# Two starts and one seam of a three-attention program: initial loads without barriers, setup and first item of the closing stream inside the batch before it

## The reference, cut to what matters

```
x = x + mla_0(layernorm(x))        # latent attention, 16 heads: the first pass of mla_sublayer
x = x + ternary(layernorm(x))      # x @ w_ste.T + bias, w_ste from round(w / mean|w|)
x = x + gated_delta(layernorm(x))  # convolved q, k, v and a recurrence over tokens
x = x + ternary(layernorm(x))
x = x + mla_1(layernorm(x))        # second pass of mla_sublayer
x = x + ffn(layernorm(x))          # the closing stream: attention that modulates a gated MLP
x = x + rotary(layernorm(x))       #                     16 heads of 16, rotary positions
x = x + ffn(layernorm(x))
```

## Time and profile before

| what | value |
|---|---|
| median of three timed runs | 3333.66 us |
| profiled execution, its own time | 3329.28 us |
| its span | 3327.5 us |
| TensorE busy | 3193.5 us, 96% |
| VectorE, ScalarE, GpSimd busy | 72%, 59%, 25% |
| DMA moved | 66.84 MB, mean 20 GB/s |

### The profile page before, as it was taken

How to read it: one execution, slowest core, us unless ns; L and a number is a source line. 1 busy time by engine, 2 the same in 40 slices (tenths; PEclk the granted TensorE clock), 3 DMA queues, 4 the chain that set the end, 5 groups by cost and what they waited for, 6 DMA issues and landing times. The chain is left out here.

```text
span 3327.5 us, 89349 instructions
## 1 busy us (share of the span) xinstructions
PE 3193.5 (96%) x34218; PEld 2639.1 (79%) x34218; DVE 2411.1 (72%) x7923; ACT 1955.1 (59%) x4769; POOL 827.1 (25%) x828
## 2 busy tenths in 40 slices
PE   6999989999999999999999969999799999999999
PEld 5888878888888888888888858788667777777787
DVE  4777778777778878787878637777666777777764
ACT  3565556666666666666666626565465555555553
POOL 2333322232222223232322223333200111111100
PEclk9999999999999999999999979999999999999999
DMA  6000000000000000000000040000000000000000
GB/s 242 1 1 1 1 8 27 22 21 18 15 18 25 18 25 18 22 16 21 21 22 21 9 163 1 1 1 1 1 1 1 1 1 1 1 5 5 5 8 10
DMA packets 51337, 66.84 MB, mean 20 GB/s; under 512 B 4962, under 2 KB 40290, under 8 KB 49378
## 3 DMA queue, kind: packets, MB, share of 16 engines
q1 hardware_dynamic: 50914, 61.13, 5.8%
HBM read 58.56 MB, written 2.56 MB: 18 GB/s over the span
## 5 line engine op out<-in xcount | busy, mean ns | idle before, releaser
L1404 DVE SCALAR_TENSOR_TENSOR d_acc<-d_raw,d_taps,d_acc 128x255 f32<-128x255 f32 x1116 | 624.0, 600 | 128.0 <-ACT d_raw L1392 114.8
L2485 ACT ACTIVATE s_probs<-s_probs,s_nmax 128x128 f32<-128x128 f32 (+1 forms) x768 | 286.8, 446 | 176.7 <-DVE s_nmax L203 176.0
L1659 ACT COPY d_power<-bank 128x768 f32<-128x768 f32 x320 | 259.5, 811 | 134.7 <-PE bank L1652 134.7
L203 DVE CUSTOM_DVE_ANT_0 s_probs<-bank,mask 128x128 f32<-128x128 f32 (+1 forms) x768 | 225.5, 349 | 105.7 <-PE bank L2466 105.6
L746 POOL TENSOR_TENSOR a_q<-a_rope 64x512 f32<-64x512 f32 x128 | 165.0, 1289 | 534.4 <-DVE a_recip L814 313.6
L1390 ACT ACTIVATE d_acc<-bank,d_tap_bias,d_taps 128x256 f32<-128x256 f32 x372 | 190.4, 563 | 148.0 <-PE bank L1368 138.2
L783 ACT ACTIVATE a_area<-a_area,a_nmax 128x128 f32<-128x128 f32 (+1 forms) x512 | 226.4, 443 | 85.6 <-DVE a_nmax L203 84.9
L203 DVE CUSTOM_DVE_ANT_0 a_area<-bank,mask 128x128 f32<-128x128 f32 (+1 forms) x512 | 159.0, 355 | 133.3 <-PE bank L764 130.9
L809 ACT COPY a_area<-bank 128x512 f32<-128x512 f32 (+1 forms) x260 | 137.3, 580 | 117.8 <-PE bank L800 117.8
L736 DVE TENSOR_TENSOR a_rope<-bank,a_sinT 32x512 f32<-32x512 f32 x256 | 177.4, 693 | 5.7
L1807 POOL TENSOR_TENSOR d_o_rs<-d_o_var,minus_half 128x4 f32<-128x4 f32 x64 | 69.6, 1088 | 419.7 <-DVE d_o_var L1801 419.7
(11 more groups left out here) (287 smaller groups left out, 8702.0 us busy)
## 6 DMA issues: line engine op xcount, KB each, us to landing
d_alpha<-d_alpha_rows SPq DMA_DIRECT2D x64, 256.0 KB, 3.6
d_g_decay<-d_running_rows SPq DMA_DIRECT2D x32, 258.0 KB, 3.5
a_w_o<-in_a_w_o SPq DMA_DIRECT2D x2, 2048.0 KB, 16.6
a_area<-in_a_q_nope SPq DMA_DIRECT2D x2, 1536.0 KB, 8.1
x<-in_x SPq DMA_DIRECT2D x8, 256.0 KB, 16.0
d_wk<-in_d_wk SPq DMA_DIRECT2D x1, 2048.0 KB
d_wq<-in_d_wq SPq DMA_DIRECT2D x1, 2048.0 KB
d_wv<-in_d_wv SPq DMA_DIRECT2D x1, 2048.0 KB
```

The lines of the kernel that those rows point to most:

```text
L203: return core.nc.vector.tensor_tensor_reduce(out=out, in0=scores, in1=core.mask[:, blocks], scale=-1.0, scalar=HIGHEST, op0=ALU.add, op1=A ...
L1404: last = nc.vector.scalar_tensor_tensor(out=convolved(G, r)[:, j, d:T], in0=raw[:, r % 2, j, 0:T - d], scalar=taps[:, r // 2, h, 3 - d:4 - ...
L1659: nc.scalar.copy(power[:], b_step[:, :, 0:3 * P]).then_inc(g.step_out, 1)
L2485: last = nc.scalar.activation(own, own, ACT.Exp, scale=-1.0, bias=nmax[:, s % 2, t, i:i + 1])
```

## The change

**The start.** `load_inputs` and `prime_signals` are gone as blocks. SP issues the first batch and the identity at the head of its list in the first pass, the mask later; each has its own semaphore, and VectorE, TensorE and the loop wait for what they need. Raising semaphores is spread: VectorE its own, TensorE 29, GpSimd one. `ident_bf` is made in the first pass's last batch.

**Two queues.** ScalarE issues, as first instructions of each pass, the tables (four now) and the ternary matrix; in the second pass it is w_ste and then the bias that come first. SP issues `early` and then `queries`, to which cosT and sinT now belong.

**The order.** `ternary_sum_pe` stands after the latent and uses bank 7. The wait for w_out moves out of `weights_ready_pe` to the first transposes of probabilities; both first projections come before `output_weights_pe`, whose fourth bank is 2 in place of 1. ScalarE copies the two first queries before w_out.

**The seam.** `mla_sublayer` of the second pass is called from inside `small_stream` with a set of functions: GpSimd sets `v` before the loop; in slots 56 to 61 (opening slots 0 to 5) each engine does, at a fixed place of its slot, its piece of the weight preparation, of the first item up to v, and of the second item's layernorm. The first item uses bank 0 instead of 7. The preparing block is gone, and the stream starts at slot 0.

```diff
         def transposes_pe(pe, n, j):
             h = 2 * n + j
+            if h == 0:
+                pe.wait_ge(g.w_out_ready, staged)
...
@@ sync, tensor
+                if after_attention:
+                    load_inputs_sp(core, sp)
                 for dst, name in early:
                     sp.dma_start(dst, ins[f"{tag}{name}"][:]).then_inc(g.small_in, 16)
-                for dst, name in tables:
-                    sp.dma_start(dst, ins[name][:]).then_inc(g.small_in, 16)
...
+                for dst, name in queries:
+                    sp.dma_start(dst, ins[name][:]).then_inc(g.queries_in, 16)
...
+                if after_attention:
+                    prime_pe(core, pe, g.prep, g.loop)
+                    pe.wait_ge(core.ident_in, 16)
...
                 prep_lat_pe(pe, -1, range(NT))
+                if after_attention:
+                    ternary_sum_pe(pe)
                 query_weights_pe(pe, 0)
                 prep_late_pe(pe, -1)
                 query_weights_pe(pe, 1)
...
-                output_weights_pe(pe)
-                weights_ready_pe(pe)
+                query_weights_ready_pe(pe)
                 project_pe(pe, 0)
                 project_pe(pe, 1)
+                output_weights_pe(pe)
...
@@ scalar
+                    act.dma_start(w_ste[:], tern.w_rows).then_inc(tern.loaded, 16)
+                    act.dma_start(t_bias[:], ins["f0_b"].rearrange("(o n) d -> o n d", o=1)
+                                  .broadcast_to([P, 1, D])).then_inc(tern.loaded, 16)
+                for dst, name in tables:
+                    act.dma_start(dst, ins[name][:]).then_inc(g.small_in, 16)
...
@@ small_stream
+        def opening_pe(pe, slot):
+            if slot == 1:
+                pe.wait_ge(*mla.latT_ready(NB - 2, 2))
+                pe.wait_ge(tern.added, 2 * NB)
+                prepare_pe(pe)
+            elif slot == 3:
+                pe.wait_ge(g.scaled_weights, 1)
+                xnT_pe(pe, 0)
+            elif slot == 4:
+                pe.wait_ge(g.scaled_weights, 2)
+                pe.wait_ge(*core.xnT_ready(item_ln(0), 1))
+                qk_pe(pe, 0, 0)
+            elif slot == 5:
+                pe.wait_ge(g.qk_ready, 1)
+                v_pe(pe, 0)
+        def opening_dve(dve, slot):
+            if slot == 0:
+                wf.wait(dve)
+                dve.wait_ge(*core.x_updated(0, 1))
+                ln_stats_dve(core, dve, item_ln(0), 0)
+            elif slot == 1:
+                normalize_dve(dve, 0)
+                modulation_weights_dve(dve)
+            elif slot == 2:
+                var2_dve(dve, 0)
+                scale_dve((wf.q, wf.k, wf.v), wf.ln1)
+                r_dve(dve, 0)
+            elif slot == 3:
+                scale_dve((wf.w_in,), wf.ln2)
+            elif slot == 4:
+                scale_dve((wf.w_up,), wf.ln2)
+                stats_dve(dve, 1)
+            elif slot == 5:
+                normalize_dve(dve, 1)
+        def opening_act(act, slot):
+            if slot == 2:
+                squares_act(act, 0)
+            elif slot == 3:
+                xnT_act(act, 0)
+            elif slot == 4:
+                wf.wait(act)
+                qk_act(act, 0, 0)
+            elif slot == 5:
+                v_evacuate(act, 0)
+        def opening_pool(pool, slot):
+            if slot == 0:
+                ln_rstd_pool(core, pool, item_ln(0))
+                pool.wait_ge(*core.ln_rstd(item_ln(0), 1))
+            elif slot == 1:
+                residual_pool(pool, 0)
+                pool.wait_ge(g.residual_added, 1)
+            elif slot == 2:
+                rms2_pool(pool, 0)
+                pool.wait_ge(g.rms2_ready, 1)
...
-        FIRST = -SETS - 1
-                for s in range(FIRST, ALL_SLOTS):
+                for s in range(ALL_SLOTS):
```

More of the change, by code:

```diff
@@ L891, in _ @@
                     w_.issue(sp)
+                if not after_attention:
+                    for w_ in following:
+                        w_.wait(sp)
                 if after_attention:
@@ L920, in _ @@
                     last_slot = n - (NB - 1) * PAIRS if after_attention else -1
+                    stream_slot = n - (NB - 1) * PAIRS if not after_attention else -1
                     if n < PAIRS_ALL:
@@ L961, in _ @@
             def _(dve):
-                if not after_attention:
+                if after_attention:
+                    prime_dve(core, dve)
+                    dve.wait_ge(core.first_tokens_in, 16)
+                else:
                     ternary_stats_dve(dve, 0)
@@ L1106, in _ @@
                 pool.wait_ge(*g.rms_ready(-1, 1))
+                if not after_attention:
+                    opening.set_up_pool(pool)
                 rope_pool(pool, 0)
@@ L1130, in _ @@
                     pool.wait_ge(*g.recip_spread(0, n + 1))
+                    if n >= (NB - 1) * PAIRS and not after_attention:
+                        opening.pool(pool, n - (NB - 1) * PAIRS)
                 if after_attention:
@@ L2742, in _ @@
             def _(pool):
-                for s in range(FIRST, SLOTS):
+                for s in range(SLOTS):
                     j, k = s // SETS, s % SETS
@@ L2805, in build @@
             w_rope = small_weights(core, weights_ctx, False)
-            mla_sublayer(core, mla, ternary, 1, [w_ffn, w_rope], None)
-            small_stream(core, w_ffn, w_rope, out)
+            small_stream(core, mla, ternary, w_ffn, w_rope, out)
 def layout(i):
```

247 lines of the change are left out of this document (126 added, 121 removed).

## The result

| | before | after |
| --- | --- | --- |
| median of the timed runs, us | 3333.67 (3332.99 to 3334.84) | 3304.07 (3297.91 to 3310.20) |
| ratio, 95% interval | | 0.9911 (0.989 to 0.9931) |
| profiled execution, us; its span | 3329.28; 3327.5 | 3297.91; 3295.8 |
| mean granted clock in it | 0.990 | 0.994 |

The forecast was 3305. The profiled one is the fastest of its four, 6.2 under the median. Spans and mean clocks of the four are 3295.8 (0.994), 3299.1 (0.991), 3304.9 (0.990) and 3308.1 (0.986).

The account below looks back on a forecast made before the run. TensorE is busy 96% of the span, so gains lie in three serial stretches: first start 9.5, second start 5.1, seam 13.9, together 28.5. 3333.66 - 28.5 = 3305 us; range 3297 to 3317.

Parts of the forecast that it names:

- First start, 9.5 predicted: First pass up to VectorE's first masked maximum: 44.9 instead of 54.36, gain 9.5 us, ends 0.5 to 13.
- The road by issue times: First start: a_rope issued at 4.0 lands 12.8 later, so with cosT and sinT query weights are there at 17.5.
- the rival of late weights: First start bound by bytes: query weights come at 22, not 17.5, 4.5 us less gain, total 3309.7; chance 0.13.
- The last step, 14.0 predicted: First start, first projection at 30.9 to first maximum at 44.9: 6.3, w_out 5.2, first scores 0.9, clock 1.6.
- Second start, 5.1 predicted: Second pass's start: 3.4 us from w_ste issued earlier plus 1.7 from the order; ends 1.6 to 5.6.
- The order, 1.7: Second start: first projection before w_out brings the maximum 1.9 us earlier, less 0.2 for ScalarE's copies.
- the 25.1 which I gave for a worthless second queue: Total gain in us, instead of 28.5, if issuing loads from a second engine saved nothing.
- Seam, 13.9 predicted: Between last batch and stream: 20.9 us removed, less 5.5 put back and 1.5 for the clock; ends 5 to 16.2.
- TensorE's own 5.0: Seam: preparation, transposes, q, k and v moved into the last batch cost TensorE their full time, 5.0 us.
- the clock's 1.5: Seam: a fall to 1.2 GHz now under the stream's first slot costs 1.5 us; ends 0 and 8.5.
- I cost 0.5: Seam: VectorE's 10.5 us just fits six slots; only opening slot 2, where r waits for GpSimd's power, costs 0.5.
- Its sign: Seam: the forecast is wrong if a slot of the last batch grows by more than its TensorE work.

Follow-up runs that it names:

- experiment 3: Changed kernel with all loads on SP's list in the order of before, no barriers: 3307.53 us, ratio 0.9924.
- after_again: The changed kernel run again without any edit: 3297.82 us, ratio 0.9891.
- ahead: Changed kernel with VectorE's scalings and two normalizations ahead of its rotary products in the last batch: 3303.55 us, ratio 0.9912.
- ahead_r: Changed kernel with VectorE's scalings and normalizations ahead of its rotary products, and r moved from opening slot 2 to slot 3: 3298.40 us, ratio 0.9893.
- fuller: Changed kernel with scalings ahead, r behind w_in's scaling, separate load waits, and idle-time transposes, also at the delta rule's end: 3284.26 us, ratio 0.9854.
- seam_back: Changed kernel with the stream opened after the last batch as before, both starts as changed: 3317.01 us, ratio 0.9953.
- experiment 5: Changed kernel with VectorE's scalings and normalizations ahead of rotary products in the last batch, r left in opening slot 2: 3303.55 us, ratio 0.9912.

## Why the prediction was right

The time was right (3304.07 for 3305): the medians differ by 29.6 for a sum of 28.5. The profiled pair differs by 31.4, since that execution is the fastest of four; its parts are what I compare, and some of them fit by luck. Step by step:

- **First start, 9.5 predicted, 9.8 found.** The steps up to the first projection came where they were put: 3.75 for 3.8, 17.25 for 17.5, 30.28 for 30.9. The road by issue times was the right one (experiment 3), and the rival of late weights fell. The last step, 14.0 predicted, took 14.26, but not in the way I had it: the sum has 6.3 up to w_out, 5.2 for it and 1.6 in reserve for the clock; both projections ran at 1.2 GHz, so it was 9.6 up to w_out, and w_out itself, behind 39.7, took 3.6. The 1.7 too little ahead of w_out and the 1.6 too much for it cancelled. after_again met the full clock earlier and came to 39.35. My ends, down to 13 of gain, were too narrow: it was 15 there.
- **Second start, 5.1 predicted, 5.15 found, by errors that cancel and a clock that I did not price.** The step that failed is "Issued first on ScalarE's list, at 1932.4, it lands by 1937.3: all 3.4 go". The product waits on one semaphore for w_ste and for the bias behind it. From first load to product it was 9.05 and is 6.74 to 6.4: 2.3 to 2.7 went, and the tables, now last on ScalarE's list, took some back at the latent product (1.10). The order, 1.7, measured 1.4. What filled the rest was the clock: it came back at 1944.5 in that execution. Where it came back at 1959.4 the whole gain of this place was gone (52.89 for 50.16).

  Before, it was low for 31.1 of the 50.16; in after for 20.6 of 45.01, in ahead for 38.2 of 49.83, in after_again for 41.4 of 52.89. Between these three, 31.1 us at 1.2 GHz would give 47.9 to 49.0, so that the change alone is worth 1.2 to 2.3 here at the clock of before (an estimate from these four profiles). Up to slot 57 another 0.6 of it is given back (374.16 from the first maximum for 373.53). I gave the clock a term at the seam and only the low end here, though before it was at 1.2 GHz for 37 us, from 1926.0 to 1963.4, ahead of the w_out that the earlier trace rows show at the full 3.67.
- **The second queue.** With one queue the first wq products are 4.05 later and the ternary product 2.45. I had put a second queue at 3.4, for w_ste alone; the first start's 9.5 rested on it as well, so that the 25.1 which I gave for a worthless second queue was too high. The Trainium skill's "usually small" (DMA: Bandwidth & Descriptors, section "Issuing engines are not separate DMA queues") holds here for one issue, some 0.47 before a landing of 12.65, and not for nine of them, which put a_rope's issue at 8.73 instead of 4.28.
- **Seam, 13.9 predicted, 12.25 found** (13.75 up to the scores, less 1.5 in the first slot). TensorE's own 5.0 and the clock's 1.5 were about right. The growth of the last batch, from the reciprocal of slot 56 to that of 63, is 7.14 (45.10 for 37.96), 5.23 with the scalings moved (ahead_r) and 4.83 with r moved as well behind w_in's (fuller); with TensorE kept busy the 1.5 is gone. The mis-sized term is "I cost 0.5" for VectorE: it is 1.9 to 2.3. Its sign came, too: slots grew by more than their TensorE work. The low end 5 that I gave this place is not the sum of its own ends (20.9 - 10.5 - 8.5 = 1.9). I had the durations of free scalings and the place of a wait for GpSimd's power. The power was not what held: r started the moment m_wv's scaling ended. What held was the scalings themselves, each pair that meets a GpSimd instruction longer by 0.8 to 1.3. The trace of before had shown it, beside the row I took w_in's 0.74 from:

```profile
2396.84 1.92 DVE L2210 TENSOR_SCALAR m_wq<-m_wq,m_ln 128x256 f32<-128x256 f32 x1 [0.32 <-PEq L870]
2398.68 0.34 DVE L2210 TENSOR_SCALAR m_wk<-m_wk,m_ln 128x256 f32<-128x256 f32 x1
```

  GpSimd set v there from 2396.80 for 1.81. One scaling of 0.34 took 1.92 and ended 0.15 behind it. The Trainium skill (SBUF — State Buffer, section "Who interferes with whom") has the rule: VectorE in its two-port modes and GpSimd share a port pair, the one that comes first keeps it for its whole instruction, and the other stands still. This case's rows agree: a stop to the other's end, not a slowdown in proportion. Both sides lose: beside m_w_in's pair GpSimd's rotary sum took 1.72 for 1.27. I did not bring it to bear.
- **Not in the sum.** 2.2 between the starts: before, a fall of 3.4 us at 468.5 cost 1.7 there, and after had none in that place; after_again took 0.6 more than before, so this is no gain of the change. In the stream 1.4, though its first slot lost 1.5: a fall at 3100.2 cost 1.7 before and nothing after, and 1.0 comes from one pair of VectorE's scalings that met GpSimd. Before, and then after:

```profile
2674.71 1.63 DVE L2278 TENSOR_SCALAR s_r<-xn,s_rms 128x256 f32<-128x256 f32 x2
2674.92 1.27 POOL L2383 TENSOR_TENSOR s_qk<-s_cosines,s_sines 128x512 f32<-128x512 f32 x1 [0.68 <-DVE s_sines L2371]
...
2645.76 0.60 DVE L2289 TENSOR_SCALAR s_r<-xn,s_rms 128x256 f32<-128x256 f32 x2
2646.26 1.27 POOL L2394 TENSOR_TENSOR s_qk<-s_cosines,s_sines 128x512 f32<-128x512 f32 x1 [0.97 <-DVE s_sines L2382]
```

  Before, GpSimd came between the two scalings and the second took 1.36; after, the second had begun at 2646.03, ahead of it, and took 0.34. That is 1.0 us, lost in before and seam_back and in none of the ten profiles with the new seam: the change gains it, and the sum had no term for it. What moved GpSimd by these 0.3 us is not shown.
- **The range**, 3297 to 3317, held the median, but executions came to 3296.06. Its ends were made of terms at one clock; the clock alone moves a start by 5 to 8.

## What to carry to other kernels

A wait on a semaphore that counts several loads ends with the last of them (1.72 and 1.10 us here); give the product its own before reordering the queue. Put VectorE's scalings from memory to memory where GpSimd has nothing to do, and count what then comes later on GpSimd's list. Where a serial stretch leaves TensorE idle between short pieces, price it at both clocks: filling the gaps with unneeded transposes was worth more here (3.3 to 9.6 us between medians) than the order of the work (1.4), and made the time repeat.

## What the hardware showed that I had not expected

- The same program's second start was granted 1.2 GHz for 10 us of its second half in one execution and for 27 in another, with TensorE busy 24.36 of those 27.2: being busy did not bring the clock back for 27 us in a stretch where transfers ran at 349 GB/s. Whether they have a part in it is open; with the gaps filled, the clock stayed up at 341 GB/s.
- In every profile of the changed kernel without filling, the clock was at 1.2 GHz from about 10 us before the second pass's first load; 42 idle-time transposes at the delta rule's end removed this wholly.
- A gap of 2.83 in the midst of a batch was followed by a fall of 3.4 us (experiment 5), where the longest gap in the changed kernel's same slots, 1.60, was followed by none.
